# A two-layer graph network on one NeuronCore: the place of four output products among the pieces of layer 1

## The reference

```python
h = jnp.maximum(_layernorm(x, axis=-1), 0.0)
x = x + _L0_gnn_ref(h, adj, ...)       # attention-weighted hops, below
h = jnp.maximum(_layernorm(x, axis=-1), 0.0)
x = x + _L1_gnn_ref(h, adj, ...)

# layer 0
e = leaky_relu(sj[:, None, :] + si[:, :, None] + ab[0], 0.2)
transition = A * exp(e) / (sum(A * exp(e), axis=-1) + 1e-12)
for k in range(3):
    H = H + Xk @ Wk[k] + bk[k]
    Xk = einsum('bij,bjd->bid', transition, Xk)
return relu(H)

# layer 1, the one that the change touches
Ah = A + eye
dh = rsqrt(sum(Ah, axis=-1))
An = dh[:, :, None] * Ah * dh[:, None, :]
out = einsum('bnm,bmf,fc->bnc', An, X, kernel) + bias
return relu(out)
```

## Time and profile before

| What | us |
|---|---|
| median of 3 runs (lowest, highest) | 786.96 (786.88, 787.1) |
| the profiled execution | 787.11 |
| its span, first to last instruction | 784.8 |
| TensorE busy | 763.4 (97%) |
| VectorE busy | 594.5 (76%) |
| ScalarE busy | 556.5 (71%) |
| GpSimd busy | 179.1 (23%) |

### The profile page before, as it was taken

The page is one execution under the profiler, slowest core; times in us unless marked ns, Lnnn a source line. Parts: engine busy times, 40 slices in busy tenths (PEclk is TensorE's granted clock), DMA queues, the critical chain, the costliest instruction groups (busy, mean ns, idle before and its releaser), DMA issues.

```text
span 784.8 us, 14253 instructions
## 1 busy us (share of the span) xinstructions
PE 763.4 (97%) x5246; PEld 702.5 (90%) x5246; DVE 594.5 (76%) x1399; ACT 556.5 (71%) x1107; POOL 179.1 (23%) x184
## 2 busy tenths in 40 slices
PE   9699999999999999999999999999999999999997
PEld 8488998989889897998979999799997999889986
DVE  6985789757886689866888568885788857894665
ACT  3989697667966779567785678857698576976351
POOL 1031240311403123030321304113040311402330
PEclk9999999999999999999999999999999999999999
DMA  7635338614477045760557505664147633365411
GB/s 236 234 116 196 125 132 290 209 75 134 144 268 243 18 151 181 253 222 1 175 198 246 188 9 182 227 237 152 67 144 257 221 119 101 133 212 180 161 62 53
DMA packets 56628, 128.58 MB, mean 164 GB/s; under 512 B 5872, under 2 KB 31856, under 8 KB 56560
## 3 DMA queue, kind: packets, MB, share of 16 engines
q1 hardware_dynamic: 47792, 97.01, 36.7%
q10 hardware_dynamic: 8768, 30.68, 11.1%
HBM read 119.28 MB, written 8.39 MB: 163 GB/s over the span
## 4 chain that ended last, share of the span: by engine, by line
PE 63%; DVE 16%; ACT 14%; POOL 3%; issue 3%; ACTq 0%; DVEq 0%; POOLq 0%
PE da L969 14%; PE acc L1103 10%; PE acc L1105 10%; PE acc L1104 9%; PE db L969 8%; ACT tg_e L457 4%; DVE t_lo L728 3%; ACT tmp L403 3%; DVE t_raw L723 3%; PE tp L1071 3%; PE tp L1073 3%; PE tp L1072 3%; ACT tg_e L463 2%; POOL hs_lo L355 2%; DVE p L754 2%
## 5 line engine op out<-in xcount | busy, mean ns | idle before, releaser
L1103 PE MATMUL acc<-g_hi,t_hi 128*128 128x256 f32 (+1 forms) x1024 | 291.3, 284 | 4.3 <-DVE g_lo L705 2.8
L1105 PE MATMUL acc<-g_hi,t_lo 128*128 128x256 f32 (+1 forms) x1024 | 289.5, 283 | 0.0
L1104 PE MATMUL acc<-g_lo,t_hi 128*128 128x256 f32 x1024 | 288.8, 282 | 0.0
L1103 PEld LDWEIGHTS acc<-g_hi,t_hi 128*128 128x128 f32 x1024 | 193.3, 189 | 5.7 <-issue 3.9
L1104 PEld LDWEIGHTS acc<-g_lo,t_hi 128*128 128x128 f32 x1024 | 193.8, 189 | 0.3
L1105 PEld LDWEIGHTS acc<-g_hi,t_lo 128*128 128x128 f32 x1024 | 193.7, 189 | 0.0
L349 POOL TENSOR_TENSOR g_lo<-tmp,g_hi 128x256 fp32r<-128x256 f32 x64 | 53.2, 831 | 276.9 <-ACT g_hi L512 276.9
L457 ACT ACTIVATE tg_e<-si,sij 128x256 f32<-128x256 f32 x256 | 109.3, 500 | 2.7 <-DVE sij L694 2.6
L734 DVE TENSOR_TENSOR a_lo<-a_raw,a_hi 128x512 fp32r<-128x512 f32 x128 | 89.7, 720 | 25.9 <-ACT a_hi L500 25.9
L344 POOL TENSOR_TENSOR rstd<-ve,mhalf 128x2 f32<-128x2 f32 (+2 forms) x41 | 51.3, 1252 | 198.3 <-DVE ve L648 149.6
L500 ACT CAST a_hi<-a_raw 128x512 fp32r<-128x512 f32 x128 | 77.1, 620 | 19.2 <-DVE a_raw L773 11.6
(11 more groups left out here) (142 smaller groups left out, 1607.2 us busy)
## 6 DMA issues: line engine op xcount, KB each, us to landing
a_raw<-adj_dram SPq DMA_DIRECT2D x64, 512.0 KB, 4.5
a_raw<-adj_z_dram SPq DMA_DIRECT2D x64, 512.0 KB, 4.2
tg_a<-adj_t_dram ACTq DMA_DIRECT2D x58, 512.0 KB, 4.0
h<-x_dram SPq DMA_DIRECT2D x32, 256.0 KB, 5.1
x_o<-x_dram SPq DMA_DIRECT2D x64, 128.0 KB, 2.5
out_dram<-x_o SPq DMA_DIRECT2D x64, 128.0 KB, 3.2
tg_a<-adj_t_dram SPq DMA_DIRECT2D x6, 512.0 KB, 3.7
p<-wk_dram SPq DMA_DIRECT2D x1, 512.0 KB, 5.7
```

The lines of the kernel that those rows point to most:

```text
L1103: nc.tensor.matmul(acc[:, s, 0:n], l_hi, r_hi, start=(jt == 0), stop=False)
L1104: nc.tensor.matmul(acc[:, s, 0:D], l_hi, r_lo, start=False, stop=False)
L1105: ins = nc.tensor.matmul(acc[:, s, 0:n], l_lo, r_hi, start=False, stop=(jt == NT - 1))
```

## The change

In the table `OUT_Z` the four output products of layer 1 that stand among its pieces follow pieces 11, 12, 13 and 14, in place of 10, 11, 12 and 13. VectorE reads the same table, so its four `out_chunk` steps move with them: to steps 12 to 15 of its loop, from 11 to 14. No instruction is added or taken away.

```diff
     NP = 2 * NT
-    OUT_Z = {10 + i: i for i in range(HJ)}
+    OUT_Z = {11 + i: i for i in range(HJ)}
     OUT_U = {1 + i: HJ + i for i in range(HJ)}
```

## The result

The median went from 786.95 to 778.96 us; the ratio is 0.9901, with a 95% interval of 0.9884 to 0.9918. The profiled execution of the changed kernel took 778.89 us, its span is 776.5; before they were 787.11 and 784.8.

The account below looks back on a forecast made before the run. TensorE was taken to set the pace, so time could come only from its gaps: 7 x 1.10 = 7.7 us off the profiled 787.11 gives 779.4, forecast median 779.3, range 778.8 to 781.2.

Parts of the forecast that it names:

- the seven waits: Layer 1, all batches but the last: output product 0 waits for DVE's subtraction at L780, 6.4 us printed in 7 times.
- The price of the stall: At product 0: later work shifts 1.10 us, start to start, against 0.84 printed idle; a restart costs 0.10 of it.
- 7 x 1.10: Whole gain: 1.10 us in each of seven layer 1 stages, 7.7 us.
- given back: Rival: DVE's lag returns at the next L780 (783.1) or wholly in aggregations (787.0); 0.09 shared with a part only, 0.04 wholly.
- The walk: TensorE's new layer 1 order, 0.71 a product and 1.40 a piece: next batch at 132.82 in place of 133.92.
- The covers: Spare time before TensorE would wait: L780 0.46, a_lo of piece 12 0.6, bank of product 3 0.8 us.
- The bank of product 3: Product 3 reuses bank db, freed by chunk 0 at 129.90 and due at 130.71: 0.8 us to spare.
- Product 4: Needs the second L780, over at 137.54, and would be due at 138.74: 1.2 us of cover.
- what is late next: Waits that could follow at TensorE: L780, a_lo of 12, bank of product 3; none before 0.46 us.
- A part only: Rival: the stall moves to another wait with little cover, gain 4.6, time 782.4; 0.09 shared with a part given back.
- The slower one: Rival: late product 3 stops DVE at chunk 3, ahead of the second L780; 788.5 and more; chance 0.03.
- The last batch: It has none of the waits and ends in a tail at L780: gain and loss nil.

Follow-up runs that it names:

- the additions: Changed kernel plus one or three extra 256-column DVE additions directly ahead of the subtraction at L780 in every batch: 780.09 and 784.48 us.
- the run with `t_low` moved: Kernel before, old product order, with DVE's t_low of unit 4 put behind L780 and one a_lo: 779.77 us, ratio 0.9904.

## Why the prediction was right

**The place and the mechanism.** TensorE sets the pace, and the seven waits were its only gaps outside start and tail. Shown: they vanish from the list, TensorE is busy throughout the stage, TensorE's order alone gives the gain and DVE's alone none, and product 0 alone is enough.

**The price of the stall.** Start to start and not by the printed idle. Shown: the stages shrink to 25.24, and the sum of the idles, 6.4, would have fallen short by 1.8 of the 8.2 that the profiled executions differ.

**The term that was a little small: 7 x 1.10.** I read the first stall and checked it against the seventh (batches 0 and 6). The stages of before stand 1.09, 1.28, 1.08, 1.28, 1.11, 1.30 and 1.09 over 25.24, 8.23 in all and not 7.7. The three odd ones cost 0.2 more:

```profile
217.33 0.39 PE L1073 MATMUL tp<-a_hi,hs_lo 128*128 128x512 f32 x1
218.75 0.39 PE L969 MATMUL db<-wl_hi,ht_hi 128*128 128x256 f32 x1 [1.03 <-DVE ht_lo L780]
```

The gap is 1.42 here and was 1.23 in the earlier trace rows. The printed 1.0 in the earlier trace rows had told of this, and I used it only for a rival. So the prediction's sentence that nothing lets the change gain more than 7.7 was wrong: it gained 8.0, and 778.96 lies only 0.16 inside the lower end of the range. The reason can be read too. TensorE's time between two stages alternates between 68.25 and 68.46, but from the end of a stage to the end of the next L780 pass 84.76 to 84.80 us in every batch, in both kernels. Before, TensorE waited for L780, so the stall took up the alternation and the period was 94.8 throughout. After the change TensorE sets it, and the periods alternate: 93.76, 93.48, 93.70, 93.51, 93.70, 93.49, on average 93.6 where 93.7 was forecast. The seven stages gave 7.89, the medians 7.99. The constant 84.8 also shows why nothing was given back: DVE's chain hangs on TensorE's stage and moved forward with it, as forecast.

**The walk.** Product 0, product 3 and the next batch were forecast at 124.38, 130.71 and 132.82 and came at 124.21, 130.55 and 132.67, all some 0.16 ahead, the part of the earlier start that was left. DVE's second L780 stayed, and its idle at the second chunk fell from 0.91 to none, as forecast.

**The covers.** Here the forecast was too generous, since each was worked out in one batch and taken for all. L780 had 0.46 in it. In the changed kernel it ends 0.27 to 0.28 before product 0 in batches 2, 4 and 6, and 0.44 and 0.46 in batches 3 and 5, where TensorE takes the longer 68.46 to come; where product 0 waited, it started 0.06 after the end of L780. That leaves 0.21 and 0.4, and the additions measured 0.20 and 0.37. The bank of product 3 had 0.8 in the forecast: the additions put t_prod from 128.45 to 129.74, with a stage that began 0.09 later, so 1.20 late, and product 3 waited 0.53, which leaves a cover of 0.67; in the changed kernel itself chunk 0 frees it 0.61 to 0.88 ahead. Product 4 had 1.2, from a start at 139.84. That figure is of the chain; TensorE's timeline, by which all other starts were read, has the product's first matmul at 139.68:

```profile
139.68 0.28 PE L969 MATMUL da<-wl_hi,ht_hi 128*128 128x256 f32 x1
```

So 1.04 was the figure to forecast, and in the changed kernel the second L780 ends 1.05 to 1.14 before product 4 in four batches and 0.85 to 0.89 in batches 2, 4 and 6. So the list of what is late next was right in its members, and the covers, counted from the printed ends as in the forecast, were up to 0.35 shorter. The forecast of the time did not hang on them.

**The rivals.** A part only, and given back: not seen, the stages are free of gaps and DVE waits for TensorE two chunks on. The slower one needed a product 3 that is late: its first half, the bank that chunk 0 frees late behind t_prod, is real and stood there once DVE was 1.0 us behind; in the changed kernel it has its margin. What product 3 late by over 4 us would do was not tried. The last batch neither gained nor lost: its tail shows the same 1.40 of wait.

## What to carry to other kernels

Where the bounding engine waits for a short chain of another one, put work that is ready between the end of its own input to the chain and the product of it; one piece of 1.40 us hid a wait of 1.3 at no cost. Price such a wait from start to start and in every repetition, since a neighbour's jitter hides in it. Then list the covers that are left: moving DVE's consumers back with the product gained nothing here, and took 1.13 us, the t_prod that now stands ahead of chunk 0, from the margin of a PSUM bank. Read each cover in several repetitions: the 0.52 of the first batch was 0.27 in the third.

## What the runs showed of the hardware that I had not expected

TensorE's clock fell after one short gap. With the products one piece earlier, the printed gap was 2.25 us in batch 0, and the matmuls behind it ran 0.42 apart instead of 0.23, with a granted clock of 0.64 over 4 us, at a cost of 1.5. It happened in three batches of seven (0.71 and 0.62 in the four us behind the gaps of batches 2 and 6), and not in the order of the gap: these two printed 2.23, while batch 1 printed 2.42 and kept 1.00. In the kernel before, with gaps up to 1.03 in this layer, it never happened. The start of the first aggregation shows the same outside this layer: all fourteen profiled executions have a printed gap of 2.77 to 2.80 us there, the first line of the list of waits above. Over the 4 us behind it nine of them granted 1.00 and five 0.57 to 0.62, and the changed kernel is on both sides, with 1.00 in one execution and 0.60 in another. The Trainium skill, page "TensorE: Matmul & The Clock Gate", part on the HAM clock gate, says that idling brings the clock down to 1.2 GHz, and that activity is watched in a window that runs free of the kernel, so that the moment of a change varies. These rows agree: mean clocks between the two levels where the clock fell, and an outcome that differs for the same kernel and the same gap.

The time between two layer 1 stages alternates by 0.2 us from batch to batch, 68.25 and 68.46. It gathers evenly along the matmuls of the second aggregation: after the change 140 of them took 16.80 us behind batch 0 and 16.62 behind batch 1, without a gap and with a granted clock of 1.00 both times. Which ones are longer differs between kernels: those ahead of the stages of batches 2, 4 and 6 before, of 1, 3 and 5 after, and of the former again in the run with `t_low` moved. I found no wait for it; its cause is open.
